# A fused attention and feed-forward kernel: the fc2 products of the last units cut into 32-row pieces, their weights placed by GpSimd, and a new order of all steps

## What is computed

```
a   = LN(x);  q = rope(a @ Wq.T);  k = rope(a @ Wk.T)        # cast to bf16
o   = sum over allowed keys of exp(q . k / sqrt(128))        # causal, one number for each position
att = relu(o * fc1_w + fc1_b) @ fc2_w.T + fc2_b              # 16 inner values, then 128
x1  = x + LN(att)
y   = relu(LN(x1) @ W1[1] + b1[1]) @ W2[1] + b2[1]           # expert 1 of 16; hidden size 256
out = x1 + LN(y)
```

## Time and profile before

| | us |
|---|---|
| median of 3 runs | 93.13 |
| lowest and highest run | 92.77, 93.20 |
| the profiled execution | 92.96 |
| span of its instructions | 91.2 |
| PE, DVE, ACT, POOL busy | 82.5, 78.5, 70.7, 59.2 |

### The profile page before, as it was taken

One profiled execution on the slowest core, in us unless ns is written; L12 is line 12 of the kernel. 1 busy time (PEld: TensorE's weight loads), 2 busy tenths in 40 slices (PEclk: granted clock), 3 DMA queues, 4 the chain that ended last, 5 costly groups with the idle time before them and its releaser, 6 DMA issues.

```text
span 91.2 us, 1530 instructions
## 1 busy us (share of the span) xinstructions
PE 82.5 (90%) x445; PEld 49.4 (54%) x445; DVE 78.5 (86%) x205; ACT 70.7 (78%) x201; POOL 59.2 (65%) x84
## 2 busy tenths in 40 slices
...
DMA packets 11884, 7.64 MB, mean 84 GB/s; under 512 B 851, under 2 KB 10980, under 8 KB 11876
## 3 DMA queue, kind: packets, MB, share of 16 engines
...
## 4 chain that ended last, share of the span: by engine, by line
PE 59%; ACT 14%; DVE 9%; DMA 7%; issue 3%; SPq 2%; POOL 2%; POOLq 1%; DVEq 0%
PE psum L724 19%; PE psum L798 14%; ACT psum L553 11%; PE psum L750 11%; PE psum L716 6%; DMA x_s<-x 4%; PE psum L777 3%; DMA qk_swap<-qk 3%; DVE rows_n L348 2%; POOL rstd L489 2%; ACT fc L566 2%; DVE qk_r L383 2%; DVE qk_swap L383 2%; PE psum L769 1%; DVE qk L505 1%
## 5 line engine op out<-in xcount | busy, mean ns | idle before, releaser
L489 POOL TENSOR_TENSOR rstd<-ve,half_neg 128x4 f32<-128x4 f32 (+2 forms) x38 | 35.0, 930 | 23.1 <-DVE ve L354 18.7
L553 ACT ACTIVATE psum<-psum 128x1024 f32<-128x1024 f32 (+7 forms) x48 | 36.6, 763 | 1.2 <-PE psum L754 0.8
L750 PE MATMUL psum<-qk_r 128*128 128x512 bf16 (+3 forms) x80 | 19.7, 348 | 1.7 <-DVE qk_r L417 1.0
L798 PE MATMUL psum<-w_c,hid 128*128 128x128 f32 x128 | 16.0, 277 | 0.0
L798 PEld LDWEIGHTS psum<-w_c,hid 128*128 128x128 f32 x128 | 15.5, 192 | 0.8 <-issue 0.3
L724 PE MATMUL psum<-cols_n,wqk 128*128 128x512 f32 (+1 forms) x36 | 15.8, 553 | 0.0
L724 PE MATMUL psum<-cols_n,w_c 128*128 128x512 f32 (+1 forms) x36 | 15.7, 550 | 0.0
L750 PEld LDWEIGHTS psum<-qk_r 128*128 128x128 bf16 x80 | 6.7, 98 | 13.0 <-ACT psum L553 4.8
L716 PE MATMUL psum<-ident,rows_n 128*128 128x128 f32 x64 | 10.2, 277 | 0.9 <-DVE rows_n L348 0.9
L638 DVE BATCH_NORM_STATS2 stats<-psum 128x6 f32<-128x256 f32 x23 | 8.7, 419 | 1.5 <-PE psum L798 1.0
L664 DVE SCALAR_TENSOR_TENSOR x<-psum,rstd,x_s 128x128 f32<-128x128 f32 x32 | 9.1, 343 | 1.0 <-POOL rstd L489 0.9
...
## 6 DMA issues: line engine op xcount, KB each, us to landing
...
```

Of the source, the lines that this page charges most:

```text
L489: ready[k].done(eng.tensor_tensor(rstd[:, g, STAT_SLOT[k], t], ve[:, g, STAT_SLOT[k], t], half_neg[:, 0:tiles], ALU.pow), n)
L553: exps.done(eng.activation(area, area, ACT.Exp, scale=scale_qk, accum_out=sums[:, g, s, j:j + 1]), n, j, s)
L750: mm = eng.matmul(psum[:, own[0] + i, 0:width], query, qk_r[:, g0 + c, 1, 0:width], start=True, stop=c < gb)
L798: mm = eng.matmul(bank[:, j * P:(j + 1) * P], hid[:, g, h, (j0 + j) * P:(j0 + j + 1) * P], w2_c[:, h, :], start=not seeded and h == 0, sto ...
```

## The change

1. **fc2 of units 5, 6, 7 and 8.** The table gives units 5 and 6 four banks each (`fc2.5#3456`, `fc2.6#3456`) and units 7 and 8 two (`fc2.7#34`, `fc2.8#12`). Each tile is then one product of 32 rows and 128 columns into a bank of its own. Units 0 to 4 keep two banks and products of 64 rows.
2. **The weights of fc2.** `+fc` is one ACT instruction of 128 partitions that writes fc2_c. A new POOL step, fcspread, makes the block diagonal out of it by two selections over 128 by 512 elements. The zeroing by DVE is gone. fc2 waits for fcspread, and `+hT` for fcmean.
3. **The order.** The whole table is new: sequence, banks, and in some 50 steps the engine. Among them, `+q.4`, `+tr1.6`, `+q.2` and `+wqk` go from ACT to DVE, `+k.3`, `+tr1.7`, `+q.8`, `+tr1.0` and eps1 of units 5 to 8 to ACT; norm1.6 goes to POOL, and norm1.1, norm1.8, cos.0, cos.5 come to DVE.

```
-load_x.4 blank.8#7 blank.1.256#7 load_x.3 mask.0 load_wqk.0 load_x.1 load_x.0 repeat.0 stat1.4 load_fc.0 eps1.4.D
...
+load_x.4 blank.10#6 blank.1.256#6 load_x.3 mask.0 load_x.6 load_wqk.0 load_fc.0 repeat.0 stat1.4 load_x.0 eps1.4.P
...
+            def spread_fc():
+
+                taken["fc"].wait(eng, 0)
+                eng.affine_select(out=fc2[:, :, :], in_=fc2_c[:, :].unsqueeze(1).to_broadcast([P, TILES, P]),
+                                  compare_op=ALU.is_ge, fill=0.0, base=0, pattern=[[-BLOCK, TILES], [0, P]],
+                                  channel_multiplier=1).then_inc(s_fc, 1)
+                eng.wait_ge(s_fc, 1)
+                fc_spread.done(eng.affine_select(out=fc2[:, :, :], in_=fc2[:, :, :], compare_op=ALU.is_ge, fill=0.0,
+                                                 base=BLOCK - 1, pattern=[[BLOCK, TILES], [0, P]],
+                                                 channel_multiplier=-1), 0)
...
                 elif name == "+fc":
                     mean_fc.wait(eng, 0)
-                    eng.wait_ge(s_zero_fc, 1)
-                    for j in range(TILES):
-                        r = slice(BLOCK * j, BLOCK * (j + 1))
-                        ins = eng.activation(fc2[r, j, :], bank_of("fc", 0)[r, P:2 * P], ACT.Identity,
-                                             bias=means[r, 2:3])
-                    taken["fc"].done(ins, 0)
+                    taken["fc"].done(eng.activation(fc2_c[:, :], bank_of("fc", 0)[:, P:2 * P], ACT.Identity,
+                                                    bias=means[:, 2:3]), 0)
...
             eng.memset(blank[:, :], 0.0).then_inc(s_blank, 1)
-            eng.memset(fc2[:, :, :], 0.0).then_inc(s_zero_fc, 1)
...
                     taken["hT"].wait(eng, n)
+                    fc_spread.wait(eng, 0)
```

More of the change, by code:

```diff
@@ L38 @@
 STEPS = """
[L39 to L52, removed]
-+k.5.D rstd3.2 scores.8.3.1#34 rope.2.D swap.5 exp.8.3.1 x1.2 cos.5.P scores.1.3.0#12 fc2.3#07 exp.1.3.0 stat4.2
@@ new lines @@
+tr1.8#2 cos.3.D +k.6.A k.1#3 load_table.4 +tr1.2.A norm1.0.D q.6#4 cos.4.D +k.1.A +tr1.8.A sin.3.D tr1.0#3 +q.6.A
+k.2#0 rope.3.D +tr1.0.A swap.6 eps1.7.A q.1#4 b2.0 sin.4.D +k.2.A scores.2.0.0#3 scores.2.1.0#2 q.0#1 rstd1.7
+load_b1.0 +q.1.A rope.4.D scores.2.3.0#0 exp.2.1.0 k.0#5 cos.6.D exp.2.3.0 rot.1#2 scores.2.2.0#4 norm1.7.P stat1.5
++q.0.A scores.3.3.0#67 exp.2.2.0 k.8#1 +k.0.A cos.1.D eps1.5.A exp.2.0.0 sin.1.D q.8#5 rstd1.5 exp.3.3.0 cos.0.D
+scores.3.2.0#23 sum.2.D +k.8.D norm1.5.P +q.8.A rot.0#4 scores.3.1.0#67 exp.3.2.0 sin.0.D swap.8 q.2#1 cos.8.D
@@ new lines @@
+exp.3.1.0 tr1.5#4 rope.1.D scores.3.0.0#23 rope.0.D +tr1.5.A hT.2#5 tr1.7#0 sin.6.D +hT.2 w1.0#6 exp.3.0.0 +q.2.D
+scores.0.2.0#5 rope.6.D scores.0.0.0#4 +tr1.7.A k.5#7 swap.2 exp.0.2.0 sin.8.D scores.5.0.0#01 +w1.0.A +k.5.D
+exp.0.0.0 q.5#5 exp.5.0.0 rope.8.D scores.0.1.0#7 sum.3.D scores.0.3.0#4 cos.2.D exp.0.1.0 scores.8.3.1#23 exp.0.3.0
++q.5.D scores.7.1.0#01 fc2.2#67 exp.8.3.1 sin.2.D swap.5 k.7#5 rope.2.D exp.7.1.0 stat3.2.D hT.3#2 scores.1.2.0#34
++hT.3 sum.0.D eps3.2.D scores.1.3.0#01 cos.5.D exp.1.2.0 q.7#2 rstd3.2 +k.7.D exp.1.3.0 sin.5.D scores.5.3.1#3
```

61 lines of the change are left out of this document (35 added, 26 removed).

## The result

The changed kernel took 94.2 us in the median of four runs (94.06 to 94.86), the kernel before on the same chip 93.16 us (four runs, 92.77 to 95.25). The ratio is 1.0149, with a 95% interval of 1.0111 to 1.0186: slower by 1.1 to 1.9%. The profiled execution took 94.86 us, with a span of 93.1 us; the 1.76 us around it are those of before.

The account below looks back on a forecast made before the run. Bound first by ACT, then TensorE. `+hT.5` ending at 62.8 us (3.7 us of ACT idle time) against a breakeven of 63.06 gave -0.26 us: 92.7 us profiled, 92.9 us on the median of 93.13; range 91.9 to 94.1.

Parts of the forecast that it names:

- the front: ACT from 5.5 to 11 us: about 3.0 us idle in place of 2.08, largely queued behind eps1.8.
- part three: New order on ACT: +1.6 us of work and 3.7 us idle, so `+hT.5` ends at 62.8 us.
- the sum: Whole kernel: 62.8 - 63.06 = -0.26 us, giving 92.9 us on the median.
- ACT ends it: Slower rival: earlier ACT idling delays fc2.5 behind `+hT.5` one to one; +1.1, 94.2 us; chance 0.22.
- the +1.6 us of work: ACT up to the end of `+hT.5`: 1.75 added net, - 1.07 of `+fc`, + 0.9 of engine changes.
- The bound of 62.2 us: Lower bound for the end of `+hT.5`, where TensorE's own work takes over: 61.78 plus 0.44 of transposes.
- the breakeven of 63.06: Start of fc2.5 on TensorE at which the kernel is as fast as before: 85.79 - 22.73 us.
- Part one: Late fc2 on TensorE: four overlapping 32-row groups take 0.41 us, 0.22 less per unit; 0.84 us gained over four units.
- Part two: fc2 weights: 1.07 us of ACT work gone at 10.3 us; two POOL selections of 0.62 us each cost zero.
- Part four: Order on TensorE: 22.73 us from fc2.5's start to the end of the first small y, in place of 24.01.
- The ropes: First rope at 17.8 us in place of 17.0; rope of unit 4 at 19.2 in place of 20.6.

Follow-up runs that it names:

- e8: Changed kernel with 12 instead of 10 filler products ahead of the wqk product and two more behind it; 92.71 us, ratio 0.9939.
- e1: Changed kernel with two filler products (512 and 256 columns) put back behind the wqk product; 92.62 us, ratio 0.9983.
- e15: Changed kernel with 12 instead of 10 filler products ahead of the wqk product, none behind it; 92.61 us, ratio 0.9945.
- e4: Kernel before with the changed kernel's front: ten fillers and a short one, x.6 loaded ahead of wqk, none behind the wqk product; 96.32 us.
- e13: The same kernel as e8, run again in another group; 92.81 us, ratio 0.9901 against the kernel before.
- e11: e8 with the fc2 weights placed by four ACT instructions again, zeroed by DVE, no POOL selections; 93.52 us, ratio 1.0053.
- e5: Changed kernel with no edit, run again in the second group; 93.71 us, ratio 1.0009 against the kernel before.
- e14: Kernel before with ten instead of eight filler products ahead of the wqk product, in the fourth group; 93.07 us, ratio 0.9979.
- e6: Kernel before with ten instead of eight filler products ahead of the wqk product, in the second group; 93.14 us.

## Why the prediction was wrong, point by point

**The step that failed** is the front in part three ("At the front there will be more of it, not less ... about 3.0 us idle from 5.5 to 11 us in place of 2.08"). It priced the queue of DVE in front of eps1.8 and took TensorE's durations there as given, those of the upper level. The diff showed that the fillers behind wqk were gone, that wqk was loaded behind x.6, and that ten fillers stood where eight had been; the sum has no term for any of them, and no rival did either. I read the fillers as work without a result. In the profiled execution ACT was idle 3.36 us up to 11 us, near the 3.0 forecast but for other reasons, and 2.18 more up to 15.3 us, in waits for TensorE that no step foresaw. Behind 11 us the sum allowed 0.7 us and 2.79 came, in all 6.15 where 3.7 were forecast; fc2.5's load started at 64.98 us for 62.8. e8, with edits of the fillers alone, lies 1.0 us below the changed kernel on one chip (e1 and e15 1.6 below, across chips), and e4 carries the loss into the kernel before.

**A second term was put at nothing**: the time outside the span, carried over as fixed. It was 1.76, 1.96, 3.3 and 2.9 us in the four executions of the result, and its cause stays open. So the late rise accounts for the profiled execution, 94.86 us, and not by itself for the median of 94.2.

**The rival that came closest** is "ACT ends it" (94.2 us). Its mechanism, that each microsecond ACT idles earlier comes through, is what happened in the profiled execution; its cause, a wait for stat1.8, is not. That its 94.2 us is the measured median is luck, since half of those executions owe their time to what lies outside the span.

**ACT's work was oversized, and so was my trust in the balance.** With the front filled (e13), ACT's listed waits up to `+hT.5` are 4.78 us, 1.1 more than forecast, and `+hT.5` still ends at 62.71 us (62.8 forecast). Some of these waits (the row at 63.11 is already behind `+hT.5`) and, last, the row of DVE that holds eps1.8 up:

```profile
7.99 0.60 ACT L521 ACTIVATE cols_n<-psum 128x512 f32<-128x512 f32 x1 [1.07 <-PE psum L727]
...
12.11 0.30 ACT L614 ACTIVATE ve<-stats,small 128x4 f32<-128x4 f32 x1 [1.44 <-DVE stats L642]
...
20.26 0.58 ACT L569 ACTIVATE psum<-psum 128x512 f32<-128x512 f32 x1 [0.28 <-PE psum L765]
22.43 0.30 ACT L614 ACTIVATE ve<-stats,small 128x4 f32<-128x4 f32 x1 [0.39 <-DVE stats L642]
63.11 0.69 ACT L569 ACTIVATE psum<-psum 128x640 f32<-128x640 f32 x1 [0.41 <-PE psum L765]
...
10.44 0.76 DVE L642 BATCH_NORM_STATS2 stats<-x_s 128x6 f32<-128x256 f32 x2 [1.65 <-DMA x_s<-x]
```

eps1.8 is waited for until 12.11 us and not 10.9. The sum had DVE busy all the way to it; in fact DVE stood idle for 1.65 us until the load of x.2 had landed (1.81 us in the changed kernel's own profile), and no term had that load. The term that was wrong on the other side is the +1.6 us of work. Counted as the prediction does, as the end of `+hT.5` less the listed waits, it is 62.71 - 4.78 = 57.93 us against 61.61 - 4.08 = 57.53: +0.4. The instructions themselves are those forecast (one more exp of 768 columns, four more eps1, three fewer of `+fc`), and ACT's busy time from 5.5 us to the end of `+hT.5` grows by 52.39 - 51.60 = 0.8 us. Another 0.4 us are gaps too short for the list, which the kernel before had (its idle time there is 4.51 us, not 4.08) and e13 hasn't. The remaining 0.8 us I can't assign. Two errors of about 1.1 us cancelled.

**fc2.5 doesn't wait for `+hT.5`.** The prediction let the end of `+hT.5` start it. In e13 the chain that ended last goes over from ACT to TensorE at 47.43 us and stays there, one product behind another, until 86.9 us:

```profile
46.39 1.04 ACT psum L569 x2
...
60.96 1.79 PE psum L810 x16
62.75 0.27 PE psum L761 x2
...
63.08 0.43 PE psum L789 x8
```

The bound of 62.2 us, where TensorE's own work would take over, was set too early: TensorE comes to fc2.5 at 63.08 us by itself. That is the breakeven of 63.06, and this execution has the span of before, 91.2 us.

**Right, with their sizes.** Part one: 0.43 and 0.42 us for an fc2 where 0.41 was forecast; the four row groups of 32 overlapped nearly in full. The Trainium skill, "TensorE: Matmul & The Clock Gate", section on packing small matmuls, gives a factor of 3.07 at 512 columns. By it, as an estimate, a four-tile fc2 would have taken 0.48 us; 0.44 and 0.43 were measured for products of 128 columns. Part two: 0.64 us for a selection (0.62 forecast), hidden; its gain on ACT is real (e11). Part four: 22.70 us, and 22.6 to 22.7 in e1, e5, e8 and e13. The sum: -0.26 us forecast, and with the fronts filled -0.26 (e13 to e14) and -0.43 (e8 to e6) in the medians, -0.48 and -0.61 in the means, 92.6 to 92.8 us for 92.9. Since two errors cancelled in it and fc2.5's start was set by something else, this agreement is luck in part. The ropes were 1.1 us later than I put them (done at 18.9 and 20.3 us in e13, 17.8 and 19.2 forecast). That had a price, if a small one: the chain of e13 runs through them to the eps1 at 22.43 us, and ACT's waits of 0.28 and 0.39 us stand there; after it ACT never waited again until `+hT.5` was done.
